# Three attention blocks of 128, 128 and 69 rows, key and query angles computed once, halves swapped by transfers

## The reference: what is computed

```python
key_phase = jnp.tanh(x @ Wk + bk) * pi
query_phase = jnp.tanh(x @ Wq + bq) * pi
...
for s in range(N_SETS):
    bound = key_ph[:, :, s, :, None] * V[:, :, None, :]
    memory = jnp.cumsum(bound, axis=1)
    retrieved = (memory * jnp.conj(qry_ph[:, :, s, :, None])).sum(axis=2).real
    total = total + weights[s] * retrieved
...
total = gate * total + (1.0 - gate) * pos_contrib
return x + total / norm @ Wo + bo
...
buf = jnp.zeros((E, CAP, d), dtype=xf.dtype).at[flat_e, pos].set(x_pairs, mode='drop')
```

## Time and profile before

| | us |
|---|---|
| median of 3 runs | 1717.03 (1716.64 to 1719.13) |
| the profiled execution's own time | 1715.9 |
| its span in the profile | 1714.0 |
| PE busy | 1519.8 (89%) |
| DVE busy | 1470.9 (86%) |
| POOL busy | 1273.1 (74%) |
| ACT busy | 1187.7 (69%) |

### The profile page before, as it was taken

How to read it: one execution, slowest core, us unless ns; L and a number is a source line. 1 busy time by engine, 2 the same in 40 slices (tenths; PEclk the granted TensorE clock), 3 DMA queues, 4 the chain that set the end, 5 groups by cost and what they waited for, 6 DMA issues and landing times.

```text
span 1714.0 us, 31340 instructions
## 1 busy us (share of the span) xinstructions
PE 1519.8 (89%) x9222; PEld 1169.7 (68%) x9222; DVE 1470.9 (86%) x6005; ACT 1187.7 (69%) x1997; POOL 1273.1 (74%) x1162
## 2 busy tenths in 40 slices
PE   2699999999999999999999999999999981776661
PEld 1477777777777777777777777777777760555551
DVE  2489999999999999999999999999999982886671
ACT  2898888888888888888888888888888740111110
POOL 0018777777777777787777777777777776688888
PEclk9899999999999999999999999999999986898885
DMA  8886666666666666665656566555555111576653
GB/s 132 216 218 140 142 140 137 132 131 124 124 118 120 112 119 112 113 111 110 110 110 111 113 112 110 112 113 113 114 113 111 42 25 45 99 114 89 101 78 34
DMA packets 259939, 193.51 MB, mean 113 GB/s; under 512 B 65514, under 2 KB 239269, under 8 KB 259785
## 3 DMA queue, kind: packets, MB, share of 16 engines
q1 hardware_dynamic: 206008, 173.23, 49.7%
q0 software_dynamic: 51200, 17.87, 8.7%
q10 hardware_dynamic: 2576, 0.60, 0.3%
HBM read 84.34 MB, written 83.73 MB: 98 GB/s over the span
## 4 chain that ended last, share of the span: by engine, by line
PE 72%; POOL 15%; issue 6%; ACT 3%; DVE 2%; DMA 1%; ACTq 1%; SPq 0%; POOLq 0%
PE bank L855 11%; POOL out_rows L602 10%; PE bank L915 8%; PE bank L932 8%; PE bank L1002 5%; PE bank L879 4%; PE bank L1010 4%; PE bank L892 4%; PE bank L863 4%; POOL slot_rows L561 3%; PE bank L974 3%; PE bank L969 2%; PE bank L964 2%; PE bank L986 2%; PE bank L953 2%
## 5 line engine op out<-in xcount | busy, mean ns | idle before, releaser
L561 POOL DMA_INDIRECT slot_rows<-xs,slot x768 | 869.3, 1132 | 241.2 <-issue 240.9
L619 ACT ACTIVATE img<-img 84x980 f32<-84x980 f32 (+1 forms) x192 | 342.2, 1784 | 17.5 <-DVE wcol L1203 13.1
L855 PE MATMUL bank<-img,w_tok 126*128 126x392 f32 (+1 forms) x640 | 224.2, 497 | 11.1 <-DMA img<-img 11.0
L602 POOL DMA_INDIRECT out_rows<-img,etok x128 | 199.5, 1559 | 30.0 <-issue 29.2
L855 PEld LDWEIGHTS bank<-img,w_tok 126*128 126x128 f32 (+1 forms) x640 | 122.9, 192 | 95.2 <-issue 14.7
L688 ACT ACTIVATE xs<-h,nb,rs 128x128 f32<-128x128 f32 x384 | 154.7, 482 | 18.4 <-DVE nb L1257 11.2
L915 PE MATMUL bank<-pos_a,v 128*128 128x325 f32 (+2 forms) x768 | 158.7, 355 | 1.3 <-ACT gt L758 1.3
L701 ACT ACTIVATE xh<-h,nb,rs 128x128 f32<-128x128 f32 x384 | 154.0, 482 | 1.0 <-DVE nb L1230 0.9
L932 PE MATMUL bank<-a_t,v 128*128 128x325 f32 (+2 forms) x768 | 152.0, 346 | 0.0
L539 POOL TENSOR_TENSOR rs<-ve,neg_half 128x6 f32<-128x6 f32 x64 | 87.3, 1365 | 81.2 <-DVE ve L1225 81.1
L915 PEld LDWEIGHTS bank<-pos_a,v 128*128 128x128 f32 (+1 forms) x768 | 125.1, 190 | 30.5 <-ACT gt L758 1.7
(11 more groups left out here) (203 smaller groups left out, 3711.0 us busy)
## 6 DMA issues: line engine op xcount, KB each, us to landing
img<-in_x SPq DMA_DIRECT2D x384, 150.1 KB
img<-img SPq DMA_DIRECT2D x256, 160.8 KB
img<-img SPq DMA_DIRECT2D x128, 128.6 KB
out_rows<-fin SPq DMA_DIRECT2D x128, 128.0 KB
slot_rows<-xs,slot POOLq DMA_INDIRECT x768
slot_rows<-init_rows SPq DMA_DIRECT2D x16, 540.0 KB, 9.5
img<-slot_rows SPq DMA_DIRECT2D x32, 270.0 KB
h<-in_txt SPq DMA_DIRECT2D x64, 128.0 KB, 2.2
```

Source lines behind the costliest of these rows:

```text
L561: g.indirect_dma_start(out=slots_d, out_offset=bass.IndirectOffsetOnAxis(ap=slot[0:nt, q.x, r, part:part + 1], axis=0), in_=xs[0:nt, q.x, ...
L602: g.indirect_dma_start(out=out, out_offset=bass.IndirectOffsetOnAxis(ap=etok[:, q.load, m:m + 1], axis=0), in_=ysum[:, q.load, m, :], in_o ...
L619: a.activation(cols[:, b0:b0 + nb, :], raw[:, q.u, :].rearrange("p (t b) -> p b t", b=P)[:, b0:b0 + nb, :], ACT.Copy)\
L855: ins = mm(bank[:, 7, 0:2 * PATCHES], w_tok[r, m, :], xk[r, k.u, :, m, :], start=(m == 0), stop=(m == SHIFT - 1))
```

## The change

1. **Blocks.** The blocks of keys have 128, 128 and 69 rows: the second takes 59 text rows more, and the third starts at row 256. So that the values' layout stays, the third block still reads the partitions of the 128 text rows, and the mask is zero for the 59 that the second has taken. The products run over 325, 197 and 69 columns in place of 325, 197 and 128. Masking becomes two instructions for a sample (325 and 266 columns) in place of one with 650.
2. **Angles.** `angles` computes 64 columns for each sample (32 keys, 32 queries), both samples side by side in one bank. ACT makes one tanh in place of two, and two distances (for sine and cosine) of it. `weighted_queries` weighs both in one instruction, and four DMAs per pair on SP (`move_halves`) carry 32 partitions of 325 numbers each to the other half of the partitions, so that keys and queries lie on the same 64. `scores` waits for them.
3. **Order.** The bodies of all five engines are in a new order, with other PSUM banks. On DVE the pipeline goes to pair k-5 in place of k-4, on PE to k-5 in place of k-3, on POOL to k-6 in place of k-4. Some semaphores of an engine on itself are left out.

```diff
+BELOW = [L - i * TILE for i in range(NT)]
+BEGIN = [sum(BELOW[0:i]) for i in range(NT + 1)]
...
+            def move_halves(q):
+                sp.wait_ge(S["a_qs"], q.count())
+                for s in range(2):
+                    lo, hi = slice(64 * s, 64 * s + 32), slice(64 * s + 32, 64 * s + 64)
+                    sp.dma_start(kq[hi, q.u, 0, :], qz[lo, q.u, 1, :]).then_inc(s_move[q.u], 16)
+                    sp.dma_start(qz[lo, q.u, 0, :], qz[hi, q.u, 1, :]).then_inc(s_move[q.u], 16)
...
-                pool.wait_ge(S["v_slot"], q.count())
+                pool.wait_ge(S["v_meta"], q.count())
...
             def scores(y):
-                pe.wait_ge(S["a_qs"], y.count())
+                wait_dma(pe, s_move, y, 4)
...
             def position_out(y, s):
-                for i, (t0, nt) in enumerate(TILES):
-                    c0 = (0, L, L + L - TILE)[i]
-                    ins = mm(bank[:, 2 + s, t0:L], v[0:nt, y.u, s, i, :], pos_a[0:nt, c0:c0 + L - t0],
+                for i in range(NT):
+                    ins = mm(bank[:, 6 + s, i * TILE:L], v[:, y.u, s, i, :], pos_a[:, BEGIN[i]:BEGIN[i + 1]],
                              start=(i == 0), stop=(i == NT - 1))
...
-            def angles_1(k):
+            def angles(k):
                 pe.wait_ge(S["a_xt"], k.count())
-                mm(bank[:, 3, 0:L], wkq[:, 1, :], x_t[:, 1, :], start=True, stop=True).then_inc(S["pe_k1"], 1)
-            def angles_0(k):
-                mm(bank[:, 2, 0:L], wkq[:, 0, :], x_t[:, 0, :], start=True, stop=True).then_inc(S["pe_k0"], 1)
+                for s in range(2):
+                    ins = mm(bank[64 * s:64 * s + 64, 4, 0:L], wkq[:, :], x_t[:, s, :], start=True, stop=True)
+                ins.then_inc(S["pe_k"], 1)
...
             def mask(y, s, done, b):
-                TT(a_t[:, s, :, :], bank[:, b:b + 2, 0:L],
-                   cst("maskn").rearrange("p (a l) -> p a l", a=2), ALU.mult).then_inc(S[done], 1)
+                TT(a_t[:, s, 0, :], bank[:, b, 0:L], cst("maskn")[:, 0:L], ALU.mult)
+                n = BELOW[1] + BELOW[2]
+                TT(a_t[:, s, 1, 0:n], bank[:, b + 1, 0:n], cst("maskn")[:, L:], ALU.mult).then_inc(S[done], 1)
```

More of the change, by code:

```diff
@@ L568, in body @@
                 p2 = k.back(2)
[L569 to L572, removed]
+                p5 = k.back(5)
+                p6 = k.back(6)
+                if p6.runs():
+                    scatter(p6, 4)
+                    scatter(p6, 5)
                 if p2.runs():
                     rstd_2(p2)
-                if p4.runs():
-                    scatter(p4, 2)
+                if p5.runs():
+                    ready(p5)
+                    scatter(p5, 0)
                 if k.runs():
                     rstd_1(k)
[L579 to L586, removed]
+                if p5.runs():
+                    scatter(p5, 1)
+                    scatter(p5, 2)
+                    scatter(p5, 3)
+            steps(body, 0, 6)
             for u in range(2):
@@ new lines, in body @@
+                if p2.runs():
+                    mask_1(p2)
+                    mask_0(p2)
+                if p4.runs():
+                    low_high(p4)
+                if p5.runs():
+                    running(p5)
+                if p1.runs():
+                    bias_scale_1(p1)
+                if p2.runs():
+                    weigh_position(p2)
+                    residual_bias(p2)
+                if p5.runs():
+                    score_low(p5)
+                if p4.runs():
+                    add_shared(p4)
+                    top_indices(p4)
+                    score_reciprocal(p4)
@@ new lines, in body @@
+                if p2.runs():
+                    weigh_sets(p2)
+                if p5.runs():
+                    score(p5)
+                if p2.runs():
+                    mix(p2)
+                if p5.runs():
+                    pick(p5)
+                if p1.runs():
+                    residual(p1)
+                if p5.runs():
+                    places(p5)
+                if k.runs():
+                    text_stats(k)
+                if p2.runs():
+                    second_rows(p2)
@@ L1499, in body @@
+                if p4.runs():
                     block_pairs(p4)
+                if k.runs():
+                    scaled_1(k)
                 if p2.runs():
[L1501 to L1514 removed]
```

418 lines of the change are left out of this document (194 added, 224 removed).

## The result

The changed kernel takes 1722.34 us (median of 7 runs, 1717.63 to 1727.67) against 1717.32 us of the kernel before (7 runs beside it): a ratio of 1.0025, with an interval of 1.0014 to 1.0037. It is a little slower, where 1699 to 1700 us had been forecast. Its profiled execution took 1723.4 us, with a span of 1721.5 us.

A forecast was written before the change was run, and what follows sets the result against it. PE's list of 21.01 us per pair was taken to bound the kernel, DVE and POOL close behind; PE falling to 19.96 leaves POOL binding at 20.49, so 17 us less: 1699 to 1700 us, range 1666 to 1719.

The forecast's parts named there:

- the four new DMAs: SP's moves behind `text`: costed at nothing, the loop summing to 18.3 us, at worst 21.3, against a turn of 20.5.
- the blocks: PE's three groups of block products: 591 columns in place of 650 save 0.22, 0.20 and 0.12 us per pair.
- PE's list, 21.01 to 19.96 us: PE's work per pair: angles and blocks save 1.09 us, taken as 1.05; 20.1 with all bounds against it.
- DVE, 20.1 us: DVE per pair: masks unchanged (upper bound 0.2 us), the new order hides tails; 20.1 us, between 19.9 and 20.3.
- case A: The forecast: POOL binds at 20.3 to 20.65 us per turn, giving 1690 to 1709 us; chance 0.43.
- the base of 20.35: POOL's own list per pair in the kernel before, with only its 13.0 us of waits on others taken off.
- rival B: POOL meets DVE's operations at better moments and fits under PE and DVE: turn 20.1 us, time 1676; chance 0.26.
- The loop by way of `scores`: From a pair's scores through DVE, `text`, stores, spreads, moves and landing to the next scores: 18.3 us, at worst 21.3.
- Fill and end, -17 us: First `ready` one DVE body later at 138.5, last at 1418.5 in place of 1435.1, so 17 us less.
- D: The moves land late, scores wait, and the deeper pipeline is left as a loss: 1729 us; chance 0.12.
- C: POOL's scatters meet DVE's operations worse: 0.3 us more per pair, turn 20.8, time 1717 us; chance 0.15.
- E: PE's narrow angle products do not run side by side: list 20.4 to 20.5 us, hidden under POOL's; chance 0.04.

The follow-up runs named there:

- run 3: The changed kernel without the four moves of a pair (its keys and queries are not the reference's): 1688.46 us, ratio 0.9829.
- run 7: The changed kernel with SP's order made `spread_2`, `spread_0`, the four moves, `text` last: 1693.48 us, ratio 0.9854.
- run 1: The changed kernel with `text` moved to stand last in SP's body, behind `spread_0`: 1697.94 us, ratio 0.9884.
- run 4: The kernel before with the blocks of 128, 128 and 69 rows alone, in the old order with the old angles: 1707.69 us, ratio 0.9945.
- run 5: run 7 with the old block widths (128, 69 and 128 rows) put back: 1700.29 us, ratio 0.9905.
- run 9: The kernel before with POOL's `ready` and scatters one body later: 1729.54 us, ratio 1.0062.
- run 2: The changed kernel with `spread_0` ahead of the four moves on SP, `text` left where it was: 1727.40 us, ratio 1.0060.
- run 10: run 7 with two of the four moves (those of the keys) issued by ACT in place of SP: 1723.51 us, ratio 1.0043.

## Why the prediction failed, point by point

The step that failed is the one on the four new DMAs: "I cost the moves at nothing: about 2 us of slack cover them". It summed one loop past the wait of `text`. Another, over `spread_0`, closes in 20.7 us and set the turn, and the moves also made the start of the pipeline later. With the moves left out, the changed kernel takes 1688.46 us and not 1722.34 (run 3). Two more terms were wrong, the blocks and POOL's list.

- **PE's list, 21.01 to 19.96 us.** Measured 20.24 us (runs 3 and 7, and most turns of run 1). The angles were right: their group and that of the logits ahead of it went from 1.79 us together to 1.25, 0.55 less, as two samples with 64 columns of weights run side by side. The blocks were the term mis-sized: 0.22 + 0.20 + 0.12 was taken in proportion to columns, 0.54 in all, and measured 0.15 (runs 4 and 5). The two together make 20.31; the last 0.07 us to 20.24 was not divided. The bound of 20.1 "with all bounds against it" was too low, since none of its bounds asked whether a pass can get arbitrarily short.
- **DVE, 20.1 us.** Right: 413.77 us busy in 420 at 20.28 per turn are 20.0 (run 1).
- **POOL's list binds at 20.49 us (case A).** Wrong. Its own list, without waits on others, measured 20.1 us in the changed kernel and 20.0 in run 1. The term that failed is the base of 20.35. It counted the 0.54 us behind the addition of `ready` as the list's own, but there `ready` had just waited for DVE:

```profile
624.70 0.19 POOL L553 TENSOR_TENSOR spare<-neg_half 128x1 f32<-128x1 f32 x1 [0.36 <-DVE slot L1350]
```

  In run 9 the same addition stands at the same place behind a scatter, has nothing to wait for, and the next scatter starts 0.16 us behind it:

```profile
624.06 0.25 POOL L553 TENSOR_TENSOR spare<-neg_half 128x1 f32<-128x1 f32 x1
624.47 1.00 POOL L561 DMA_INDIRECT slot_rows<-xs,slot  x1 [0.16 <-issue]
```

  So some 0.37 us of the gap goes with the late places and not with the list; why late places leave the longer gap is not shown. (A turn earlier DVE had finished them 0.16 us ahead of the addition, and the next scatter still started 0.51 us behind it.) Without it the base is 20.0, and with the forecast's +0.14 the list is 20.1, as measured. What the scatters lose to DVE stayed what it was (all twelve last 13.65 us before and 13.63 in run 1), as the forecast took; a lock of this kind, of which the prediction cites the rule, stands in the changed kernel's timelines of POOL and DVE, where a scatter begins within `residual_bias`:

```profile
616.25 1.78 POOL L582 DMA_INDIRECT slot_rows<-xs,slot  x1 [0.30 <-issue]
```

```profile
616.19 0.95 DVE L1393 TENSOR_TENSOR hbo<-hbo,bo_row 128x768 f32<-128x768 f32 x1
```

  It could have come out better: in runs 2, 5 and 10 the twelve last 12.8, 12.7 and 12.8 us, which is the better meeting of rival B, but in none of them did POOL set the turn.
- **The moves at nothing.** Wrong at two places. The loop by way of `scores` was summed well: 18.3 forecast, 19.0 by run 2, with moves at 0.6 us each where 0.4 was taken. But it was not the only loop through the wait of `text`. The one over `spread_0`, its landing of 3.5 us, and ACT was never summed, and at 20.7 it was the longer. The prediction listed the moves' own reader and not the others that are queued behind `text` on SP. The second place is the fill, where the moves cost 7 us (run 3).
- **Fill and end, -17 us.** The depth itself was right in kind: one body deeper is a turn later at the start (run 9, where the end gives back a third of it). The first `ready` was forecast at 138.5, and came at 149.2. Some 5 of the 10.7 us are the moves (144.5 without them). The rest, 6.0 us, stands in the traces of before and of run 3. With the moves left out, `places` of the first pair starts at 138.42 for 116.91 before, 21.5 us later and not a body of 20.3. `slot` starts 5.2 us behind it and not 1.3, since it stands later in DVE's body. And `ready` starts 0.9 us behind `slot`, as it stands on POOL behind `rstd_2`, whose variance comes late in the fill; the forecast had put it at `slot` itself. The rows of run 3:

```profile
143.62 0.16 DVE L1360 TENSOR_TENSOR slot<-slotf,over 128x12 int32<-128x12 f32 x1
```

```profile
143.18 1.32 POOL L563 TENSOR_TENSOR rs<-ve,neg_half 128x6 f32<-128x6 f32 x1 [14.45 <-DVE ve L1263]
144.47 0.45 POOL L572 TENSOR_TENSOR spare<-neg_half 128x1 f32<-128x1 f32 x1
```

- **The rivals.** D (1729) is nearest in time and in kind, transfers behind `text` that come late and nearly take PE's gain. But in the changed kernel `scores` didn't wait for them in the steady turn, and its price was reckoned for another ring. C and A didn't occur. E named a PE list of 20.4 to 20.5, but through the angles, which were right. B's turn of 20.1 comes near that of run 1; its time of 1676 is 22 us under it, 13 of them at the first `ready`, the rest in the turns.
- **1699 us and run 1.** That run 1 takes 1697.9 us is two errors that cancel: from the first to the last `ready` it takes 1265.8 us and not 1280 (14 less), and its first `ready` comes at 151.8 and not 138.5 (13 more). That the time agrees is luck.
- **Where the gain went.** PE's list fell by 0.77 us per pair, 45 us over 58 turns. The ring through SP gave back 0.48 us of it in each turn, 28 us (run 1, whose first `ready` is 2.6 us later, takes 24 us less). The start of the pipeline took 26. The sum is 9 us more, and 7.5 were measured.

## What to carry to other kernels

When a wait stands in a queue with transfers behind it, sum every loop that passes that wait, not only that of the transfers you add; and try first to put the waiting instruction last. A product shortened from 128 to 69 columns need not save what its columns promise: here 0.15 us of 0.54 per turn were saved (runs 4 and 5). A deeper pipeline costs about one turn per body at the start, of which the last turns gave back a third here (run 9), and every transfer added to a turn is paid in the fill even where the steady turn hides it.

## What the runs showed of the hardware

- A float32 pass of 69 columns steps on after 62 ns, a second one right behind it after 110; passes of 128 columns take 109 to 113 (run 4 and the kernel before).
- A transfer within SBUF costs SP's queue 0.6 us to issue (32 partitions) or 0.8 us (42 partitions, `spread`), and landed 2.2 (run 2), 3.5 (changed kernel) and 4.4 us (run 7, in the fill) later; its issue on ACT costs 0.6 us in ACT's own order (run 10).
- A scatter on POOL starts 0.16 to 0.17 us behind a small addition that had nothing to wait for, whether a root (run 1) or a scatter (run 9) stood before it, and 0.5 us behind one whose awaited places DVE had only just finished (the kernel before). Behind another scatter it starts 0.30 us late in all of them.
